# GpSimd's tap pairs after the shared taps' low part, picked rows split inside the last gates, second GELU first

## What is computed

```python
h = relu(bn(conv1d(xc, conv1_w, 0))); h = bn(conv1d(h, conv2_w, 8))     # 17 taps
x_conv = relu(h + xc)
A = exp(-dist) * mask; x_nmp = A @ relu(x @ w_msg.T + b_msg)
r, z = sigmoid(gi_r + gh_r), sigmoid(gi_z + gh_z)                       # GRU on [x_conv, x_nmp] and x
x = x + (1 - z) * tanh(gi_n + r * gh_n) + z * ln(x)
# feed-forward, on the 511 nodes of each graph with the largest router weight
w = ln(x) @ wr; sel = rows of ln(x) with the 511 largest w
y = (gelu(sel @ w1 + b1) @ w2 + b2) * w_sel                             # 128 -> 512 -> 128
x = x + (y in its rows) + ln(x)
```

## Time and profile before

| | us |
|---|---|
| median of 3 runs | 564.93 (564.66 to 565.52) |
| profiled execution | 564.87 |
| its span in the trace | 562.3 |
| outside the span | 2.57 |
| PE busy | 545.6 |
| DVE busy | 475.0 |
| ACT busy | 354.9 |
| POOL busy | 275.7 |

### The profile page before, as it was taken

One profiled execution on the slowest core, in us unless ns is written; L12 is line 12 of the kernel. 1 busy time (PEld: TensorE's weight loads), 2 busy tenths in 40 slices (PEclk: granted clock), 3 DMA queues, 4 the chain that ended last, 5 costly groups with the idle time before them and its releaser, 6 DMA issues.

```text
span 562.3 us, 9026 instructions
## 1 busy us (share of the span) xinstructions
PE 545.6 (97%) x2964; PEld 416.6 (74%) x2964; DVE 475.0 (84%) x1048; ACT 354.9 (63%) x616; POOL 275.7 (49%) x346
## 2 busy tenths in 40 slices
PE   7799999999999999999999999999999999899996
PEld 3786798678966896689767986798678966666663
DVE  6987478679898989899898989899979987978722
ACT  4856475856686577747674857575856673555552
POOL 2740354325358344834484546654545365536552
PEclk9999999999999999999999999999999999899999
DMA  8602700180008300650047001800171006402111
GB/s 274 278 2 76 300 0 2 45 308 23 2 0 270 142 2 1 193 220 1 1 124 289 1 2 52 323 2 1 46 283 46 1 1 191 148 16 81 36 36 61
DMA packets 33339, 54.52 MB, mean 97 GB/s; under 512 B 2098, under 2 KB 23051, under 8 KB 33166
## 3 DMA queue, kind: packets, MB, share of 16 engines
q1 hardware_dynamic: 29710, 48.42, 24.7%
q0 software_dynamic: 3584, 5.54, 2.8%
HBM read 44.21 MB, written 13.43 MB: 103 GB/s over the span
## 4 chain that ended last, share of the span: by engine, by line
PE 86%; DVE 8%; ACT 3%; DMA 2%; issue 1%; SPq 0%; DVEq 0%; ACTq 0%
PE N L1504 20%; PE M L1481 10%; PE C L1355 7%; PE C L1357 7%; PE C L1356 7%; PE D L1475 5%; PE N L1609 5%; PE N L1355 4%; PE N L1356 3%; PE N L1357 3%; ACT hab L674 2%; DVE tr L1014 2%; PE M L1356 2%; PE M L1355 2%; PE M L1357 2%; PE D L1355 2%
## 5 line engine op out<-in xcount | busy, mean ns | idle before, releaser
L780 ACT ACTIVATE tr<-D 128x512 f32<-128x512 f32 x128 | 76.4, 597 | 76.9 <-PE D L1475 75.2
L1481 PEld LDWEIGHTS M<-cst,adjb 128*128 128x128 f32 x512 | 63.9, 141 | 35.2 <-issue 21.2
L1475 PE MATMUL D<-V,U 128*128 128x512 f32 x128 | 89.3, 698 | 0.0
L1481 PE MATMUL M<-cst,adjb 128*128 128x128 f32 x512 | 76.8, 273 | 0.6 <-DVE ga L1101 0.6
L578 POOL DMA_INDIRECT sel<-R,ridx x56 | 61.1, 1090 | 16.0 <-issue 14.0
L1504 PE MATMUL N<-ga,msgF 128*128 128x512 f32 x128 | 64.2, 594 | 0.0
L1504 PE MATMUL N<-tz,msgF 128*128 128x512 f32 x128 | 64.2, 594 | 0.0
L1355 PE MATMUL C<-zR,wc 128*128 128x256 f32 x208 | 60.6, 291 | 0.6 <-DVE zR L1023 0.6
L1356 PE MATMUL C<-zR,wc 128*128 128x256 f32 x208 | 58.7, 282 | 0.0
L1357 PE MATMUL C<-zR,wc 128*128 128x256 f32 x208 | 58.6, 282 | 0.0
L1131 DVE TENSOR_SCALAR_CACHE_REDUCE junk<-W,R 128x1024 bf16<-128x1024 f32 (+3 forms) x64 | 51.7, 808 | 3.9 <-ACT W L742 3.9
(11 more groups left out here) (236 smaller groups left out, 1527.6 us busy)
## 6 DMA issues: line engine op xcount, KB each, us to landing
adjb<-in_adj SPq DMA_DIRECT2D x8, 4096.0 KB, 14.9
adjb<-sel SPq DMA_DIRECT2D x7, 516.0 KB, 5.3
xall<-in_x SPq DMA_DIRECT2D x7, 512.0 KB, 5.2
out<-R SPq DMA_DIRECT2D x7, 512.0 KB, 3.5
R<-in_conv_w SPq DMA_DIRECT2D x1, 1088.0 KB, 8.6
sel<-R,ridx POOLq DMA_INDIRECT x56
xall<-in_weights SPq DMA_DIRECT2D x1, 832.0 KB, 11.0
xall<-in_x SPq DMA_DIRECT2D x2, 256.0 KB, 2.9
```

What stands on the lines that cost most here:

```text
L780: nc.scalar.activation(E[:, u % NE, :], Db[u % NH][:, :], ACT.Exp, scale=-1.0).then_inc(exp_ok, 1)
L1475: MM(Db[h][:, :], U[:, t * P:(t + 1) * P], V[:, half(h)], start=True, stop=True).then_inc(d_ps, 1)
L1481: i = TR(Mb[h][:, k * P:(k + 1) * P], adjb[:, h * TH + k, t * P:(t + 1) * P], ident)
```

## The change

Five edits.

1. In the opening `pairs_of_taps` on GpSimd waits until the low part of `W_SC` is there (`wL_ok` at 2).
2. The first layer norm's statistics are taken in two halves of four tiles, each with its own mean, variance and power on GpSimd. `conv1` on PE orders its three matmuls so that the low part of the input is read last.
3. The first group's rows are transposed inside the last batch's second gates (bank M0 in place of D0), their high part stands ahead of those gates on ACT, and their low part ahead of `rank(6, 5)` on DVE.
4. `up_banks` begins with D1, so that the first three `up` wait for gates that are read earlier.
5. The second GELU stands ahead of the high part of the second group on ACT; its low part moves ahead of `rank(6, 7)` and of the last `blend` on DVE; `state_back` of the last batch moves two `down` later on PE.

```diff
-        up_banks = (C0, C1, D1)
+        up_banks = (D1, C0, C1)
@@ gpsimd
                 if first:
+                    pool.wait_ge(wL_ok, W_SC + 1)
                     pairs_of_taps()
@@ scalar
                 gates(b, 0)
                 candidate(b, 0)
+                if last:
+                    hi_of_sel(0, 0)
                 gates(b, 1)
...
             def ffn_step(b, q, first, last):
-                if first:
-                    hi_of_sel(0, 0)
                 gelu(b, q, 0)
                 if first:
                     candidate(B - 1, 1)
+                gelu(b, q, 1)
+                if first:
                     hi_of_sel(1, 1)
-                gelu(b, q, 1)
                 gelu(b, q, 2)
@@ gpsimd, the powers of the first norm
-                pool.wait_ge(agg, 1)
                 for h, done in ((0, rstd0_ok), (1, rstd_ok)):
+                    pool.wait_ge(agg, h + 1)
@@ vector
+            def moments0(h):
+                dve.wait_ge((x0_in, x_in[0])[h], 16)
+                moments1_of(0, range(h * TH, (h + 1) * TH))
+                mean_and_variance(0, stats1, (h + 1) * TH, slice(h * TH, (h + 1) * TH), h)
...
-            moments1(0)
-            mean_and_variance(0, stats1, T)
+            moments0(0)
+            moments0(1)
             normalise0()
...
                 blend(b, 0)
                 if last:
+                    lo_of_sel(0, 0)
                     rank(b - 1, 0, 5)
...
                     new_gate(B - 1, 1)
-                    lo_of_sel(0, 0)
                     rank(B - 2, 0, 6)
+                    lo_of_sel(1, 1)
                     rank(B - 2, 0, 7)
                     indices(B - 2, 0, 1)
                     blend(B - 1, 1)
-                    lo_of_sel(1, 1)
                     state_to_nodes(B - 1, (M1, N1))
@@ tensor
-                    wait(pe, xTL_ok, b, NH, h + 1)
-                    three(Db[h][:, :], weight(W_C1), xTH[:, q, half(h)], xTL[:, q, half(h)],
-                          True, True).then_inc(c1_ps, 1)
+                    w, hs = weight(W_C1), half(h)
+                    wait(pe, xTH_ok, b, NH, h + 1)
+                    MM(Db[h][:, :], w(0), xTH[:, q, hs], start=True, stop=False)
+                    MM(Db[h][:, :], w(1), xTH[:, q, hs], start=False, stop=False)
+                    wait(pe, xTL_ok, b, NH, h + 1)
+                    MM(Db[h][:, :], w(0), xTL[:, q, hs], start=False, stop=True).then_inc(c1_ps, 1)
...
                 three(nh[:, :], wh(2), *X, True, True).then_inc(gate_ps, 1)
+                if last and h == 1:
+                    sel_to_features(0)
                 three(ni[:, :], wi(2, 0), *XC, True, False)
...
-                    sel_to_features(0)
                     for k in range(LU):
                         up(0, 0, k)
...
                     if first and j == 0:
                         sel_to_features(1)
+                    if first and j == 1:
+                        up(1, 1, 0)
+                    if first and j == 2:
                         pe.wait_ge(tz_ok, NH * (B - 1) + 1)
                         pe.wait_ge(ga_ok, NH * B)
                         state_back(B - 1, (M1, N1))
-                    if first and j == 1:
-                        up(1, 1, 0)
```

More of the change, by code:

```diff
@@ L823, in gates, with hi_of_sel @@
                 nc.scalar.activation(tz[:, h, :], z[:, :], ACT.Tanh, bias=col(V_GB + 1), scale=0.5).then_inc(tz_ok, 1)
+            def hi_of_sel(b, p):
+                wait(act, t_ps, b, 1, 1)
+                nc.scalar.activation(xTH[:, 0, half(p)], sel_bank(b)[:, :], ACT.Copy).then_inc(xsH_ok, 1)
             def candidate(b, h):
@@ L923, in _, with moments1_of @@
             TS, TT, STT = nc.vector.tensor_scalar, nc.vector.tensor_tensor, nc.vector.scalar_tensor_tensor
+            def moments1_of(b, ts):
+                for t in ts:
+                    nc.vector.bn_stats(st[:, 0, t, :], xall[:, b % NX, t, :]).then_inc(stats1, 1)
             def moments1(b):
@@ L928, in moments1 @@
                     dve.wait_ge(rstd_ok, b)
[L929 to L934, removed]
+                dve.wait_ge(x_in[b % 2], 16 * (b // 2 + 1))
+                moments1_of(b, range(T))
+            def moments0(h):
+                dve.wait_ge((x0_in, x_in[0])[h], 16)
+                moments1_of(0, range(h * TH, (h + 1) * TH))
+                mean_and_variance(0, stats1, (h + 1) * TH, slice(h * TH, (h + 1) * TH), h)
             def moments2(b):
@@ L940, in moments2, with mean_and_variance @@
                     nc.vector.bn_stats(st[:, 1, t, :], xall[:, b % NX, t, :]).then_inc(stats2, 1)
-            def mean_and_variance(k, stats, n):
-                (me, mo), (ve_, vo) = ((st[:, k, :, i], st[:, k, :, i + 3]) for i in (1, 2))
+            def mean_and_variance(k, stats, n, ts, turn):
+                (me, mo), (ve_, vo) = ((st[:, k, ts, i], st[:, k, ts, i + 3]) for i in (1, 2))
                 dve.wait_ge(stats, n)
[L946 to L954, removed]
+                TT(msum[:, ts], me, mo, ALU.add)
+                TT(mdif[:, ts], me, mo, ALU.subtract)
+                TS(vsum[:, ts], ve_, 1.0 / D, EPS, ALU.mult, ALU.add).then_inc(mom1, 1)
+                dve.wait_ge(mom1, turn + 1)
+                TS(mean[:, ts], msum[:, ts], 0.5, None, ALU.mult)
+                STT(mdif[:, ts], mdif[:, ts], 0.25, mdif[:, ts], ALU.mult, ALU.mult)
+                STT(vsum[:, ts], vo, 1.0 / D, vsum[:, ts], ALU.mult, ALU.add).then_inc(mom2, 1)
+                dve.wait_ge(mom2, turn + 1)
+                TT(ve[:, ts], vsum[:, ts], mdif[:, ts], ALU.add).then_inc(agg, 1)
             def normalise0():
@@ L1036, in common_added, with lo_of_sel @@
                 STT(phases(GS[k]), on_phases(cc), col(V_SC2), phases(G1), ALU.mult, ALU.add).then_inc(gs_ok, 1)
+            def lo_of_sel(b, p):
+                wait(dve, xsH_ok, b, 1, 1)
+                TT(xTL[:, 0, half(p)], sel_bank(b)[:, :], f32(xTH[:, 0, half(p)]), ALU.subtract).then_inc(xsL_ok, 1)
             def new_gate(b, h):
@@ L1443, in conv_odd, with sel_to_features @@
                 i.then_inc(c2_ps, 1)
+            def sel_to_features(b):
+                if b < NXS:
+                    pe.wait_ge(sel_in[b], 16)
+                else:
+                    pe.wait_ge(xn2_ok, B)
+                if b == 0:
+                    pe.wait_ge(tr_ok, NH * (B - 1) + 1)
+                if b == 1:
+                    pe.wait_ge(q2_ok, NH * (B - 1) + 1)
+                wait(pe, xsL_ok, b - 1, 1, 1)
+                for c in range(TH):
+                    rows = Xs[:, b, c, 0:D] if b < NXS else R[:, 1, (b - NXS) * TH + c, 0:D]
+                    i = TR(sel_bank(b)[:, c * P:(c + 1) * P], rows, ident)
+                i.then_inc(t_ps, 1)
             def state_back(b, bank_):
@@ L1574, in _ @@
             over_batches(pe, step)
[L1577 to L1588, removed]
             def up(b, p, j):
@@ L1593, in up @@
                 if k < LU:
[L1594 removed]
+                    pe.wait_ge((ga_ok, tr_ok, tz_ok)[k], NH * B if k > 0 else NH * (B - 1) + 1)
                 else:
```

12 lines of the change are left out of this document (4 added, 8 removed).

## The result

The changed kernel takes 567.25 us (566.83 to 568.21, 7 runs) where the kernel before takes 564.93 (564.38 to 565.52, 7 runs): ratio 1.0043, 95% interval 1.0032 to 1.0054. It is slower by 2.4 us, more than the 0.2% that can be told from no change. Its profiled execution took 567.3 us, with a span of 565.5: 1.8 us lie outside the span, against 2.57 in the profiled execution of before.

What follows compares the result with a forecast made beforehand. PE was taken to bound the kernel, busy 545.6 of 562.3 us, so its stalls count. 564.87 + 1.85 (opening) + 1.5 (clock) - 1.2 (feed-forward), edit 2 at 0, gave 567.0 us; range 563.0 to 568.5.

Steps and rivals of the forecast that it cites:

- The opening stall: Opening: late tap pairs delay ACT's list to common_part, so PE stalls about 4.2 us before conv_even_common; costs 1.85 us.
- the turns: Opening: DVE and GpSimd alternate on their shared port, each waiting out the other's whole instruction, about 1.1 us per turn.
- Edit 2: Opening: halved statistics and conv1's new order were taken to be worth 0 us, at most some 0.3 later.
- ACT's start of the chain is set by a DMA: Opening: ACT's first weight pass waits for in_conv_w at 11.87 after 0.28 us idle, so earlier statistics gain nothing.
- The clock: Behind the opening's stall: clock falls to its lower level for 3.4 us, costing 1.5 us, bounds 0 to 1.7.
- rival (a): After the opening's stall the clock holds, giving 565.5 us; chance 0.23.
- Rival (b): Opening: ports favour GpSimd, pairs precede W_S's low part, cost 0.2 us; feed-forward part keeps 2.0; 563.1 us, chance 0.17.
- the split: Opening: were the shared port a split of bandwidth, DVE and GpSimd could overlap and the cost be near 0.2 us.
- The feed-forward part: Start of the feed-forward part: its stall goes, DVE's serial work hides much of that; gain 1.2 us, bounds 0 to 2.0.
- the moments' slip: Feed-forward part: the last moments on DVE finish 0.3 us later, at about 499.65, and last_norm starts 0.65 earlier.

Runs made afterwards that it cites:

- e3: Changed kernel plus eight matmuls, result unread, on PE in the opening's stall before conv_even_common; 564.91 us, 1.0008 of the kernel before.
- e5: e3 with edit 2 undone (statistics whole, conv1's old order); 566.22 us, 1.0027 of the kernel before.
- e1: Kernel before with edit 1 alone (GpSimd's tap pairs wait for W_SC's low part); 568.57 us, 1.0070 of the kernel before.
- e2: Changed kernel without edit 1, edits 2 to 5 kept; 564.00 us, 0.9992 of the kernel before.
- e4: Changed kernel with both embeddings and common_part ahead of W_PAIRS's high part on ACT in the opening; 564.89 us, 1.0003 of the kernel before.
- e6: e4 with add_msg_bias ahead of W_PAIRS's low part on DVE in all batches; 563.81 us, 0.9989 of the kernel before.
- e8: e6 with DVE's low part of rank 7 ahead of the second transposed half's low part; 564.56 us, 0.9992 of the kernel before.
- e9: e4 with five extra matmuls, result unread, in the opening's PE stall; 564.22 us, 0.9989 of the kernel before.
- e10: e6 with three extra matmuls, result unread, in the opening's PE stall; 564.08 us, 0.9993 of the kernel before.
- e11: e7 with three extra matmuls, result unread, in the opening's PE stall; 565.00 us, 1.0004 of the kernel before.
- e7: e6 with edit 5 undone, edits 3 and 4 kept; 564.94 us, 1.0010 of the kernel before.

## Why the prediction was right, point by point

**567.0 was forecast and 567.25 measured; the opening and the clock came as forecast, two of the four terms did not, and that the sum is off by only 0.25 us is in part luck.** In the span the changed kernel is 3.2 us longer, where the terms made +2.15.

*The opening stall, +1.85.* Right in its mechanism to each step, as the rows of after show: W_S's low part went ahead of the first pair on DVE, the turns alternated, ACT's list shifted whole (20.64 to 26.36, 5.72 us where 5.75 was read), and `common_part` ended the stall. Measured +1.50. From W_SC's low part on the turns took 3.90 us (16.70 to 20.60), where 3.85 was worked out (17.05 to 20.9). W_SC was there 0.35 earlier than forecast: with edit 2 GpSimd's list began 0.68 earlier (13.67 against 14.35), and one DVE instruction more, L1026 with 0.34, then fell behind GpSimd's turn.

*Edit 2, 0.* Wrong. The step that failed is "ACT's start of the chain is set by a DMA", because it took the landing of one execution for a fixed time. In the trace of before the convolution's weights land 8.6 us after their issue and ACT waits 0.28 us for them. In the changed kernel's they land after 7.6, and L843 follows at once, at 11.19 in place of 11.87: 0.29 of that is ACT's pass before it, which starts at 10.71 in place of 11.00, and 0.39 the landing. In the 13 profiled executions the landing took 6.4 to 8.6 us, so before's is the longest. In e3 it took 8.2, and ACT waited again although edit 2 is in:

```profile
11.50 1.06 ACT L844 ACTIVATE wc<-R 128x1024 fp32r<-128x1024 f32 x1 [0.61 <-DMA R<-in_conv_w]
```

The edit is worth 0.57 (e5 against e3), outside the bounds of 0 to 0.3, which had left out a gain.

*The clock, +1.5.* Right: 1.51 in the changed kernel, 1.52 in e1, 0 in e3, where only PE's idle time was taken away. The rival (a), 565.5, needed the clock to hold; in the 7 runs of the changed kernel it did not. (Its mean clock was 0.993 to 0.996 in all of them, e3's 0.999 to 1.000. Before's runs have 0.992 to 0.997 as well, from falls elsewhere, such as the one at 489 us; so it is e3 that places this one behind the opening's stall.) Rival (b) fell at the point named: DVE's low part of W_S, queued already, came first, and L554, started at 16.70, took 2.20 us with the wait for its turn in it. DVE's L1035 then took 1.77 us, where an instruction of its shape takes 0.69 at 26.50. This is what "an exclusive lock, not a bandwidth split" says (the Trainium skill, "SBUF — State Buffer", section "SBUF: two separate sides"); by the split the opening would have cost near 0.2.

*The feed-forward part, -1.2.* Half of it was there, and in the changed kernel none. Without the 3.19 us of shift, the second low part made PE wait 0.55 (0.7 forecast), state_back 0.91 (1.1), and `up` of the third group is at 500.72: 1.55 ahead of before, where 2.0 was forecast. What failed is the size of the moments' slip: 0.68 us at POOL's power (503.33 - 3.19 = 500.14 against 499.46), not 0.3. So last_norm is 0.28 earlier and not 0.65, DVE's list behind it holds PE for 0.46 at the weights' row, where the sum had no wait, and at 517.28 (520.47 - 3.19) the gain is 0.59. That is what the stretch shows in e2, e3 and e4: 83.91 to 84.01 against 84.58, a gain of 0.6 to 0.7 us in place of 1.2.

*The late row update.* In the changed kernel that gain is lost again. DVE's third block of updated rows starts after 1.34 us of idle time (the row at 523.36 above), where it is 0.75 in the trace of before, and a later `up` of PE waits 0.52. The same 0.6 to 0.8 us is missing in e5, e6, e8, e9 and e10 and not in e2, e3 and e4. Between e4 and e9 only five PE instructions in the opening differ:

```profile
519.60 1.13 DVE L1300 SCALAR_TENSOR_TENSOR xn<-M,adjb 128x128 f32<-128x128 f32 x4 [0.75 <-PE M L1641]
```

```profile
520.30 1.13 DVE L1301 SCALAR_TENSOR_TENSOR xn<-M,adjb 128x128 f32<-128x128 f32 x4 [1.48 <-PE M L1645]
```

The first is e4's and the second e9's. The transposes that the row reads are at 518.96 and 518.94, so DVE had the same input at the same time. The row also waits until the rows of the first group have left their buffer (`out_done`), but the last of those DMAs lands near 515 us in both, so that is not it. Nor was DVE alone late. The GELU on ACT that reads the matmuls at 517.3 us (the last of the three starts at 517.87 in e4 and 517.85 in e9) stands in e4 and e9 at:

```profile
518.31 0.69 ACT L900 ACTIVATE xall<-C,vec 128x512 f32<-128x512 f32 x1 [0.95 <-PE C L1372]
```

```profile
520.22 1.27 ACT L901 ACTIVATE xall<-C,vec 128x512 f32<-128x512 f32 x2 [2.90 <-PE C L1373]
```

Both wait for a semaphore that PE raises, and the traces' semaphore records show when it went up. In e4 the GELU's (`f1_ps`) goes up 0.02 us after its matmul ends, at 518.28, and in e9 (whose trace lacks some of these records, but not these) 1.96 us after it, at 520.20; that of DVE's row (`yb_ps`) goes up 0.02 after the last transpose, at 519.58, and 0.74 after it, at 520.28. In the changed kernel the two delays are 1.11 and 0.61. In the six kernels with the late row `yb_ps` goes up 0.61 to 0.83 us after the transposes' end, in the other seven 0.01 to 0.02, but for e11's 0.14. So what is late is PE's signal that its work is done, and not an input of DVE. Why PE's signal comes late there in some kernels stays open; no experiment was made on it. It belongs to a kernel and not to a run as far as e9's and e4's runs tell (564.1 to 564.6 in all of e9's, 563.4 to 563.6 in those of e4 with a full clock).

*What balances.* Of the span's 3.2 us: 1.50 the stall (2.07 by the wait, less 0.57 by edit 2), 1.51 the clock, 0.18 that came in between the first `front` and the last gates and has no row that names it, and 0.02 for the feed-forward part. In time it is 2.4, since the 2.57 us outside the span of before's profiled execution were 0.6 to 0.8 more than in most of its other runs, and its span of 562.3 was 0.1 to 0.5 us shorter than theirs (medians of 562.4 to 562.8 beside the experiments). A sum made against that execution inherited 0.8 us that had nothing to do with the change. Forecast and result agree to 0.25 us because of that and of the opening, which cost 0.35 less than forecast; the two stood against the 1.2 us of gain that did not come. That part is luck.

**A version without the loss.** e6 (0.9989), e9 (0.9989) and e10 (0.9993) are 0.6 to 0.4 us faster than the kernel before and 3 us faster than the changed one. Against the kernel before that is less than the 0.2% taken as measurable, though the first two intervals lie below 1. They keep edit 1 and take `common_part` out from behind it.

## What to carry to other kernels

When a wait is added on one engine, follow the list of every engine behind it to the last thing it issues: here a wait that saved PE 2.6 us at once held a copy eight passes down ACT's list, and moving that copy ahead of the waiting pass gave all of it back. A stall of the matmul engine of 2 to 4 us costs its length and often some of the clock behind it; here several stalls of up to 0.91 us left the clock alone (the changed kernel near 495 us) where one of 3.44 took it down (e11). A few matmuls in the stall whose result is not read are a quick test of how much is clock. A gain read at one point is only worth what the serial engine behind it lets through; sum it at the end of that engine's list, with each chain hop in it.

## What the runs showed that was not expected

- Stalls of the same length take the clock down in one execution and not in the next. Behind 2.53 us in e4's opening it fell in 7 of 11 runs, behind 1.78 us in e6's in 2 of 11, behind 1.76 us of the same opening in e7's and e8's profiles in both, behind 3.43 us at 491 in e7's profile not at all and in e11's for 3.4 us, behind 3.97 us in the changed kernel in all 7. In e9 and e10, which keep PE at work through the opening's stall, every run has a mean clock of 0.997 or more. The numbers of runs go by the times and mean clocks; e3, e9 and e10, with the stall filled, show that it was this stall. Each fall measured in a profile lasted 3.4 us, or in e2's twice that.
- One DMA of the same size, issued at 3.2 to 3.3 us each time, lands 6.4 to 8.6 us later from one profiled execution to the next. A wait of 0.28 us behind it in one trace differs from run to run and is not a bound.
- Five instructions more on PE at 23 us went with 0.7 us at 520, in a place that none of them touches. There a semaphore of PE went up 0.7 to 2.0 us after the work that it reports.
